# First sublayer of a long kernel: the inverse levels and u and w as 128-row products on a block diagonal

## The chip, the cores and the metric

The kernel runs on one core of one Trainium2 chip. The metric is the device time of one execution in microseconds, the median of several runs; less is better. Within the core, TensorE (PE; its weight loads are listed as PEld), VectorE (DVE), ScalarE (ACT), GpSimd (POOL) and SyncE (SP) each work through a queue of their own and meet at semaphores.

## The reference, cut to what matters

The reference is a chain of twelve sublayers, each followed by a layer norm. The change lies in the first, a gated delta rule over 4 batches, 256 times and 4 heads of 32 channels, in chunks of 32 times:

```python
A = jnp.where(tri_strict, -(kbc @ jnp.swapaxes(kc, -1, -2)), 0.0)
M = eye - A
T = solve_triangular(M, jnp.broadcast_to(eye, M.shape), lower=True)
u = T @ vc
w = T @ kbc
...
def step(S, inp):                      # over the 8 chunks
    attn = jnp.where(causal, q_i @ jnp.swapaxes(k_i, -1, -2), 0.0)
    u_adj = u_i - w_i @ S
    o_i = q_i @ S + attn @ u_adj
    return (S + jnp.swapaxes(k_i, -1, -2) @ u_adj, o_i)
```

So for each of 8 chunks, 4 batches and 4 heads, 128 small problems in all, a 32x32 unit lower triangular matrix is inverted, and the inverse is applied to v and k.

## The kernel before, in words

The program goes through the sublayers one after another. The first, `gated_delta`, has three parts, each closed by a barrier of all engines (`Place.close`, L66): `delta_project` (projections, convolutions and filters), `delta_inverse` (the part that changes) and `delta_scan` (the loop over the chunks).

In `delta_inverse` the 8 chunks are two groups g of four chunks; each group has four PSUM banks, `ps[g]`. Rows of a tile are (batch b, time i), its columns (head h, time j) or (h, channel), each 4 times 32. The order on every engine is the order of the code. The steps:

- Three sets of 8 transposes (L690) and their evictions on ScalarE (L747) give k, kb and vb with times in the rows.
- The Gram products (L698, L700): for every chunk, head and batch two 32x32 TensorE products, 128 per group. ScalarE copies `raw` (L750), GpSimd multiplies it by a mask for each of four levels into `A_s` (L767), VectorE makes the first `invT` (L775 to L778).
- Four levels. In each, for g = 0 and 1: four transposes of `invT` (L707), 64 products `A_s` by `invT` of 32x32 (L713); ScalarE evicts the turned `inv` (L754) and the product `M1` (L755); then for g = 0 and 1 64 products `inv` by `M1` (L722), and VectorE adds them to `invT` (L783), which the next level waits for.
- u: 64 products of 32x32 for each group (L731). w: 64 more (L739). ScalarE (L757, L758) and VectorE (L785, L786) evict one group each.

Every fp32 product of the code shows as two MATMUL and two LDWEIGHTS records in the trace, every transpose as one of each. In the trace the tiles are called `tiles_...` (this part), `delta_...` (shared by the three) and `scan_...`; `tiles_M` is `M1`.

`delta_scan` follows with 16 products of 32x32 each for the state (L856), the output (L862), w (L844) and q (L849) of every chunk; VectorE updates u (L902) and the state (L906, at first L908).

Of the kernel before, what the change touches and what calls it, by code (L numbers as in the profile page):

```python
# [633 lines left out]
def delta_inverse(m, kT, kqT, vbT, u, k, wT, attnT):  # L634
# [5 lines left out]
    LEVELS = 5  # L640
    with ExitStack() as ctx:
# [7 lines left out]
        M1 = place.sbuf("M1", [P, CH, P])  # L649
# [8 lines left out]
        A_ready = place.counter("A_ready")  # L658
        invT_ready = place.counter("invT_ready")
        M_made = place.counter("M_made")  # L660
        M_ready = place.counter("M_ready")
        U_made = place.counter("U_made")
        u_made = place.counter("u_made")
# [10 lines left out]
        def out_of(g, lo, hi):  # L674

            return ps[g][:, :, lo:hi].rearrange("p h (c j) -> p c h j", j=32)

# [9 lines left out]
        def _(pe):  # L687
# [4 lines left out]
            for g in range(2):  # L692
# [9 lines left out]
                mm.then_inc(grams_made.sem, 1)  # L702
            for s in range(1, LEVELS):
                for g in range(2):
                    pe.wait_ge(invT_ready.sem, invT_ready.nth(2 * (s - 1) + g + 1))
                    for n, c in enumerate(of(g)):
                        pe.transpose(ps[g][:, n, 2 * P:3 * P], invT[:, c, :], m.ident[:, :])  # L707
                    pe.wait_ge(A_ready.sem, A_ready.nth(2 * (s - 1) + g + 1))
                    for n, c in enumerate(of(g)):
                        for b in range(B):  # L710
                            for h in range(H):
                                on, to = slice(32 * b, 32 * b + 32), slice(32 * h, 32 * h + 32)
                                mm = pe.matmul(ps[g][to, b, 32 * n:32 * n + 32], A_s[on, s, c, to], invT[on, c, to], start=True, stop=True,  # L713
                                               skip_group_check=True)
                    mm.then_inc(M_made.sem, 1)
                for g in range(2):
                    pe.wait_ge(M_ready.sem, M_ready.nth(2 * (s - 1) + g + 1))
                    for n, c in enumerate(of(g)):
                        for h in range(H):
                            for b in range(B):  # L720
                                on, to = slice(32 * h, 32 * h + 32), slice(32 * b, 32 * b + 32)
                                mm = pe.matmul(ps[g][to, h, P + 32 * n:P + 32 * n + 32], inv[on, c, to], M1[on, c, to], start=True, stop=True,  # L722
                                               skip_group_check=True)
                    mm.then_inc(U_made.sem, 1)
            for g in range(2):
                pe.wait_ge(invT_ready.sem, invT_ready.nth(2 * (LEVELS - 1) + g + 1))
                for n, c in enumerate(of(g)):
                    for h in range(H):
                        for b in range(B):
                            on, ch = slice(32 * b, 32 * b + 32), slice(32 * h, 32 * h + 32)  # L730
                            mm = pe.matmul(ps[g][on, n, ch], invT[on, c, ch], vb[on, c, ch], start=True, stop=True, skip_group_check=True)  # L731
                mm.then_inc(u_made.sem, 1)
            for g in range(2):
                pe.wait_ge(u_made.sem, u_made.nth(g + 1))
                for n, c in enumerate(of(g)):
                    for b in range(B):
                        for h in range(H):
                            on, ch = slice(32 * b, 32 * b + 32), slice(32 * h, 32 * h + 32)
                            mm = pe.matmul(ps[g][ch, b, P + 32 * n:P + 32 * n + 32], kb[on, c, ch], invT[on, c, ch], start=True, stop=True,  # L739
                                           skip_group_check=True)  # L740
                mm.then_inc(w_made.sem, 1)

        @block.scalar
        def _(act):
# [3 lines left out]
            for g in range(2):  # L748
                act.wait_ge(grams_made.sem, grams_made.nth(g + 1))
                act.activation(by32(raw, g), out_of(g, 0, P), ACT.Copy).then_inc(raw_ready.sem, 1)  # L750
            for s in range(1, LEVELS):
                for g in range(2):
                    act.wait_ge(M_made.sem, M_made.nth(2 * (s - 1) + g + 1))
                    act.activation(inv[:, 4 * g:4 * g + 4, :], ps[g][:, :, 2 * P:3 * P], ACT.Copy)  # L754
                    act.activation(by32(M1, g), out_of(g, 0, P), ACT.Copy).then_inc(M_ready.sem, 1)  # L755
            act.wait_ge(w_made.sem, w_made.nth(1))
            act.activation(u[:, 0:4, :], ps[0][:, :, 0:P], ACT.Copy)  # L757
            act.activation(by32(wT, 0), out_of(0, P, 2 * P), ACT.Copy)  # L758

        @block.gpsimd  # L760
        def _(pool):
            pool.wait_ge(const_in.sem, const_in.nth(32))
# [7 lines left out]
        def _(dve):  # L770
            dve.wait_ge(const_in.sem, const_in.nth(32))
            for g in range(2):
# [6 lines left out]
                                  ALU.add).then_inc(invT_ready.sem, 1)  # L779
            for s in range(1, LEVELS):  # L780
                for g in range(2):
                    dve.wait_ge(U_made.sem, U_made.nth(2 * (s - 1) + g + 1))
# [3782 lines left out]
```

## Time and profile before

| | us |
|---|---|
| median of three runs | 3913.87 |
| lowest, highest | 3901.09, 3919.18 |
| the profiled execution, its own time | 3946.06 |
| its span in the trace | 3944.3 |
| mean granted TensorE clock in it | 0.892 of full |
| `delta_inverse`, first transpose to last copy | 99.1 to 195.1 |

All starts are microseconds from the start of the span. A row in order of time gives start, length, engine, line, tiles, the count of instructions merged in it, and in brackets how long the engine had been idle before and what ended that. "issue" there means that the engine waited for nothing that the profile shows. In tables of stretches PEclk is the granted clock as a share of full: 1.00 is 2.4 GHz, 0.50 is 1.2 GHz. The lengths of MATMUL records are modelled and overlap, so that the starts tell more than the ends.

### The profile page before, as it was taken

What the parts mean: (1) busy time and instruction counts of PE and PEld (TensorE: products, weight loads), DVE (VectorE), ACT (ScalarE), POOL (GpSimd) and SP (SyncE); (2) the same over time, 40 slices, a digit from 0 to 9 for tenths busy, and PEclk for the clock granted to TensorE, in tenths of its full rate; (3) what the DMA queues carried; (4) which work ended last, traced back from release to release, by engine and by line L of the source; (5) the groups of instructions that cost most, each with busy time, mean ns of one, the idle gap of its engine ahead of it and who ended that gap; (6) DMA issues with size and microseconds to landing.
All of it is one profiled execution on the core that took longest, in us unless ns stands there. A gap on an engine that the chain in (4) does not pass through costs nothing. (4 is left out here: it accounts for less than half of the span.)

```text
span 3944.3 us, 96221 instructions
## 1 busy us (share of the span) xinstructions
PE 3325.7 (84%) x40498; PEld 2328.4 (59%) x40498; DVE 2616.4 (66%) x4510; ACT 1952.2 (49%) x3525; POOL 1267.1 (32%) x842
## 2 busy tenths in 40 slices
PE   7566697999999998766649668999999988999996
PEld 4445665777777776731123345666666665667774
DVE  5124385666666666379977777888888864567773
ACT  1122344655555554359961234566665652345553
POOL 1101303555555553410021236655666631000000
PEclk9577888999999999788868889999999996789997
DMA  1021501000000000810000211111111101000000
GB/s 40 6 63 50 166 1 39 1 10 1 10 1 1 1 1 8 257 58 1 1 5 1 60 58 44 48 54 42 51 52 42 26 21 40 9 19 20 11 2 11
DMA packets 88726, 131.40 MB, mean 33 GB/s; under 512 B 18450, under 2 KB 60106, under 8 KB 87532
## 3 DMA queue, kind: packets, MB, share of 16 engines
q1 hardware_dynamic: 85292, 119.03, 10.6%
q8 instruction: 324, 5.31, 0.6%
q0 software_dynamic: 3008, 6.23, 0.4%
q14 instruction: 102, 0.84, 0.1%
HBM read 86.63 MB, written 10.94 MB: 25 GB/s over the span
## 5 line engine op out<-in xcount | busy, mean ns | idle before, releaser
L2786 POOL TENSOR_TENSOR wide_probs<-wide_probs,wide_factor 128x1024 f32<-128x1024 f32 x128 | 239.6, 1893 | 311.1 <-ACT wide_factor L2747 311.1
L2743 ACT ACTIVATE wide_probs<-wide_ps_s,wide_nm 128x1024 f32<-128x1024 f32 (+1 forms) x256 | 237.2, 927 | 172.6 <-DVE wide_nm L2828 152.8
L175 POOL TENSOR_TENSOR model_Y<-model_Y,model_X 128x512 f32<-128x512 f32 x12 | 15.2, 1268 | 942.4 <-POOLq L66 942.4
L2294 ACT ACTIVATE narrow_probsT<-narrow_ps 128x512 f32<-128x512 f32 (+1 forms) x448 | 220.1, 582 | 136.0 <-PE narrow_ps L2198 133.6
L2823 DVE TENSOR_REDUCE wide_nm<-wide_ps_s 128x1 f32<-128x1024 f32 x128 | 156.0, 1219 | 193.6 <-PE wide_ps_s L2629 193.6
L2348 DVE TENSOR_REDUCE narrow_part<-narrow_ps 128x1 f32<-128x512 f32 x384 | 242.4, 685 | 52.6 <-PE narrow_ps L2181 50.2
L3933 POOL TENSOR_TENSOR local_turn<-local_turn 128x1024 f32<-128x1024 f32 x96 | 226.7, 2369 | 157.0 <-DVE local_turn L3991 156.8
L3147 DVE TENSOR_TENSOR bonds_strain<-peri_in_moved 128x1664 f32<-128x1664 f32 (+3 forms) x128 | 257.0, 2085 | 1.0 <-PEq L66 1.0
L3198 PE MATMUL bonds_ps<-bonds_act_of,bonds_out 128*32 128x448 f32 (+3 forms) x1024 | 153.5, 697 | 117.9 <-ACT bonds_act_of L3171 83.9
L2181 PE MATMUL narrow_ps<-second_KQ 32*128 32x512 f32 x768 | 247.2, 668 | 1.1 <-ACT second_KQ L2265 1.0
L2641 PE MATMUL wide_ps<-model_ident,wide_probs 128*128 128x128 f32 (+1 forms) x1664 | 238.9, 274 | 10.8 <-DVE wide_probsT L2833 9.1
L2833 DVE COPY wide_probsT<-wide_ps 128x512 f32<-128x512 f32 x256 | 173.7, 686 | 84.8 <-PE wide_ps L2641 84.0
L2198 PE MATMUL narrow_ps<-narrow_Q,second_KQ 32*128 32x256 f32 (+1 forms) x1664 | 227.8, 396 | 0.0
L2629 PE MATMUL wide_ps_s<-wide_KQ 64*128 64x512 f32 (+1 forms) x1024 | 212.3, 531 | 9.9 <-ACT wide_probs L2743 9.0
L2641 PEld LDWEIGHTS wide_ps<-model_ident,wide_probs 128*128 128x128 f32 (+1 forms) x1664 | 193.3, 139 | 42.7 <-DVE wide_probsT L2833 13.6
L3942 POOL TENSOR_TENSOR local_turn<-local_turn,local_ss 128x1024 f32<-128x1024 f32 x96 | 184.1, 1918 | 82.5 <-ACT local_ss L3877 82.5
L3814 PE MATMUL local_ps<-e_wqkv,local_xs 128*128 128x512 f32 x384 | 193.0, 627 | 4.9 <-DVE local_xs L3965 4.3
L2653 PE MATMUL wide_ps<-wide_probsT,wide_V 128*64 128x128 f32 (+1 forms) x3328 | 195.9, 275 | 0.9 <-DVE wide_probsT L2833 0.9
L2198 PEld LDWEIGHTS narrow_ps<-narrow_Q,second_KQ 32*128 32x128 f32 (+1 forms) x1664 | 175.2, 182 | 25.6 <-DVE narrow_part L2348 7.7
L2653 PEld LDWEIGHTS wide_ps<-wide_probsT,wide_V 128*64 128x64 f32 (+1 forms) x3328 | 180.5, 137 | 5.4 <-DVE wide_probsT L2833 1.1
L3198 PEld LDWEIGHTS bonds_ps<-bonds_act_of,bonds_out 128*32 128x32 f32 x1024 | 25.4, 123 | 240.5 <-ACT bonds_act_of L3171 179.2
L2629 PEld LDWEIGHTS wide_ps_s<-wide_KQ 64*128 64x128 f32 x1024 | 93.4, 187 | 95.1 <-issue 93.3
(643 smaller groups left out, 8452.0 us busy)
## 6 DMA issues: line engine op xcount, KB each, us to landing
moe_w<-in_L_ffn_w SPq DMA_DIRECT2D x62, 512.0 KB
local_V<-local_V SPq DMA_DIRECT2D x96, 128.0 KB
e_wqkv<-in_L_ffn_qkv SPq DMA_DIRECT2D x6, 1536.0 KB, 7.2
local_V<-local_V SPq DMA_DIRECT2D x144, 64.0 KB
context_rows<-in_ctx SPq DMA_DIRECT2D x8, 768.0 KB
e_keys<-in_ctx_T SPq DMA_DIRECT2D x6, 800.5 KB, 4.9
e_source<-in_ctx_T SPq DMA_DIRECT2D x4, 800.5 KB, 4.4
second_source<-in_ctx_T SPq DMA_DIRECT2D x4, 800.5 KB, 5.7
```

What stands on the lines that cost most here:

```text
L2181: mm = pe.matmul(bank[:, 0:hi - lo], Qh[:, t * P:(t + 1) * P], Kh[:, lo:hi], start=True, stop=True)
L2198: mm = pe.matmul(bank[0:hi - lo, at:at + q1 - q0], KQ_of(s)[part_of(h), lo:hi], Q2[part_of(h), s % RING, q0:q1], start=True, stop=True, sk ...
L2294: act.activation(probsT[0:high, c % PROBS, h, 0:wide], bank[0:high, 0:wide], ACT.Exp).then_inc(t_taken_act.sem, 1)
L2348: dve.tensor_reduce(part[:, s % 2, t, h, piece:piece + 1], bank[:, :], AX.X, ALU.min).then_inc(s_taken.sem, 1)
L2629: mm = pe.matmul(ps_s[h][:, j * BANK:j * BANK + c1 - c0], KQ[rows, s % 2, pair, K + tile * P:K + (tile + 1) * P], KQ[rows, s % 2, pair, c0 ...
L2641: mm = pe.transpose(bank[0:high(c), j * P:(j + 1) * P], probs[:, n % 2, h, c * P:c * P + high(c)], m.ident[:, :])
L2653: mm = pe.matmul(bank[64 * h:64 * h + 64, 0:P], V[0:high(c), s % 2, c, 128 * pair + 64 * h:128 * pair + 64 * h + 64], probsT[0:high(c), n ...
L2743: act.activation(probs[:, n % 2, h, lo:hi], ps_s[h][:, 0:hi - lo], ACT.Exp, bias=nm[:, n % 2, h, 2 * half:2 * half + 1], scale=1.0, accum_ ...
L2786: pool.tensor_tensor(v, v, factor[:, n // 4 % 2, j:j + 1].broadcast_to([P, CUT]), ALU.mult).then_inc(lowered[i].sem, 1)
L3147: dve.tensor_tensor(out, window, here, ALU.subtract).then_inc(strain_dve.sem, 1)
L3814: mm = pe.matmul(slot[:, j, :], xs[:, b, WIN + u * P:WIN + (u + 1) * P], wqkv[:, i, at + j * BANK:at + (j + 1) * BANK], start=True, stop=True)
L3933: pool.tensor_tensor(turn1[:, n % 2, j, :, :], turn1[:, n % 2, j, :, :], turn2[:, j, :, :], ALU.add)
```

## The change

The two products of each level, and u and w, are formed by contracting over all 128 rows. For that, one operand is held four times as wide, with its 32-row pieces set apart on a block diagonal and zeros elsewhere. `invT4[:, c, h, :]` is 128x128 and holds head h's four batch pieces of `invT`; `M4[:, c, b, :]` likewise holds the product. GpSimd clears both tiles once (two memsets of 128x4096 fp32).

- Each level's first product is 16 products per group instead of 64, of `A_s[:, s, c, ch]` (128 rows, 32 columns, stationary) with `invT4[:, c, h, :]` (128 columns, moving), all to bank MID of the group. The second is 16 of `inv[:, c, on]` with `M4[:, c, b, :]`, all to bank OUT. The transposes of `invT` stay and go to bank TURN.
- Filling the tiles that are set apart is new work: after every update of `invT`, VectorE copies the pieces b = 0, 1 and ScalarE the pieces b = 2, 3, for each group; after every first product, VectorE copies h = 0, 1 out of PSUM into `M4` and ScalarE h = 2, 3. Each copy has 32 partitions of 512 elements. They take the place of the eviction of `M1`, one instruction of 128 partitions.
- u is formed turned (`uT`), 16 products per group, evicted by VectorE, turned back with four transposes per group, and evicted again. w is 16 products per group, and its eviction is a plain copy.
- The Gram products and the scan are as they were.

The core of the diff:

```diff
+        invT4 = place.sbuf("invT4", [P, CH, H, P])
+        M4 = place.sbuf("M4", [P, CH, B, P])
+        uT = place.sbuf("uT", [P, CH, P])
+        def bank(g, k):
+            return ps[g][:, k, :].rearrange("p (c x) -> p c x", x=P)
+        def apart(v, g, i):
+            own = slice(32 * i, 32 * i + 32)
+            return v[own, 4 * g:4 * g + 4, :, own]
+        def parts(v, i):
+            return v[32 * i:32 * i + 32].rearrange("p c (x j) -> p c x j", j=32)
...
         def _(pe):
+            def against_invT4(g, k, left):
+                for n, c in enumerate(of(g)):
+                    for h in range(H):
+                        ch = slice(32 * h, 32 * h + 32)
+                        mm = pe.matmul(bank(g, k)[ch, n, :], left[:, c, ch], invT4[:, c, h, :], start=True, stop=True, skip_group_check=True)
+                return mm
             for s in range(1, LEVELS):
                 for g in range(2):
                     pe.wait_ge(invT_ready.sem, invT_ready.nth(2 * (s - 1) + g + 1))
                     for n, c in enumerate(of(g)):
-                        pe.transpose(ps[g][:, n, 2 * P:3 * P], invT[:, c, :], m.ident[:, :])
+                        mm = pe.transpose(bank(g, TURN)[:, n, :], invT[:, c, :], m.ident[:, :])
+                    mm.then_inc(inv_made.sem, 1)
                     pe.wait_ge(A_ready.sem, A_ready.nth(2 * (s - 1) + g + 1))
-                        for b in range(B):
-                            for h in range(H):
-                                on, to = slice(32 * b, 32 * b + 32), slice(32 * h, 32 * h + 32)
-                                mm = pe.matmul(ps[g][to, b, 32 * n:32 * n + 32], A_s[on, s, c, to], invT[on, c, to], start=True, stop=True,
+                    pe.wait_ge(invT4_dve.sem, invT4_dve.nth(2 * (s - 1) + g + 1))
+                    pe.wait_ge(invT4_act.sem, invT4_act.nth(2 * (s - 1) + g + 1))
+                    against_invT4(g, MID, A_s[:, s]).then_inc(M_made.sem, 1)
+                for g in range(2):
+                    pe.wait_ge(inv_ready.sem, inv_ready.nth(2 * (s - 1) + g + 1))
+                    pe.wait_ge(M4_dve.sem, M4_dve.nth(2 * (s - 1) + g + 1))
+                    pe.wait_ge(M4_act.sem, M4_act.nth(2 * (s - 1) + g + 1))
                     for n, c in enumerate(of(g)):
                         for b in range(B):
+                            on = slice(32 * b, 32 * b + 32)
+                            mm = pe.matmul(bank(g, OUT)[on, n, :], inv[:, c, on], M4[:, c, b, :], start=True, stop=True, skip_group_check=True)
                     mm.then_inc(U_made.sem, 1)
...
+                against_invT4(g, OUT, vb).then_inc(uT_made.sem, 1)
+                against_invT4(g, MID, kb).then_inc(w_made.sem, 1)
+            for g in range(2):
+                pe.wait_ge(uT_ready.sem, uT_ready.nth(g + 1))
                 for n, c in enumerate(of(g)):
+                    mm = pe.transpose(bank(g, TURN)[:, n, :], uT[:, c, :], m.ident[:, :])
...
         def _(act):
+            act.wait_ge(cleared.sem, cleared.nth(2))
+            def spread_invT(s, g):
+                act.wait_ge(invT_ready.sem, invT_ready.nth(2 * s + g + 1))
+                for b in range(2, B):
+                    ins = act.activation(apart(invT4, g, b), parts(group(invT, g), b), ACT.Copy)
...
         def _(pool):
+            pool.memset(invT4[:, :, :, :], 0.0).then_inc(cleared.sem, 1)
+            pool.memset(M4[:, :, :, :], 0.0).then_inc(cleared.sem, 1)
...
         def _(dve):
+            for g in range(2):
+                spread_invT(g)
             for s in range(1, LEVELS):
                 for g in range(2):
+                    dve.wait_ge(M_made.sem, M_made.nth(2 * (s - 1) + g + 1))
+                    for h in range(2):
+                        ins = dve.tensor_copy(apart(M4, g, h), parts(bank(g, MID), h))
+                    ins.then_inc(M4_dve.sem, 1)
+                for g in range(2):
                     dve.wait_ge(U_made.sem, U_made.nth(2 * (s - 1) + g + 1))
-                    dve.tensor_tensor(by32(invT, g), by32(invT, g), out_of(g, P, 2 * P), ALU.add).then_inc(invT_ready.sem, 1)
+                    dve.tensor_tensor(group(invT, g), group(invT, g), bank(g, OUT), ALU.add).then_inc(invT_ready.sem, 1)
+                    spread_invT(g)
```

On TensorE, the last level and u and w of the kernel before (`ps0` and `ps1` are the banks of the two groups, a count is of products of the code, and the shape is that of the result, partitions by columns):

```order
L707 MATMUL tiles5_ps0<-model1_ident,tiles5_invT 128x128 x4
L713 MATMUL tiles5_ps0<-tiles5_invT,tiles5_A_s 32x32 x64
L707 MATMUL tiles5_ps1<-model1_ident,tiles5_invT 128x128 x4
L713 MATMUL tiles5_ps1<-tiles5_invT,tiles5_A_s 32x32 x64
L722 MATMUL tiles5_ps0<-tiles5_M1,tiles5_inv 32x32 x64
L722 MATMUL tiles5_ps1<-tiles5_M1,tiles5_inv 32x32 x64
L731 MATMUL tiles5_ps0<-tiles5_vb,tiles5_invT 32x32 x64
L731 MATMUL tiles5_ps1<-tiles5_vb,tiles5_invT 32x32 x64
L739 MATMUL tiles5_ps0<-tiles5_invT,tiles5_kb 32x32 x64
L739 MATMUL tiles5_ps1<-tiles5_invT,tiles5_kb 32x32 x64
```

The same place in the changed kernel:

```order
L741 MATMUL tiles5_ps0<-model1_ident,tiles5_invT 128x128 x4
L734 MATMUL tiles5_ps0<-tiles5_invT4,tiles5_A_s 32x128 x16
L741 MATMUL tiles5_ps1<-model1_ident,tiles5_invT 128x128 x4
L734 MATMUL tiles5_ps1<-tiles5_invT4,tiles5_A_s 32x128 x16
L754 MATMUL tiles5_ps0<-tiles5_M4,tiles5_inv 32x128 x16
L754 MATMUL tiles5_ps1<-tiles5_M4,tiles5_inv 32x128 x16
L734 MATMUL tiles5_ps0<-tiles5_invT4,tiles5_vb 32x128 x16
L734 MATMUL tiles5_ps0<-tiles5_invT4,tiles5_kb 32x128 x16
L734 MATMUL tiles5_ps1<-tiles5_invT4,tiles5_vb 32x128 x16
L734 MATMUL tiles5_ps1<-tiles5_invT4,tiles5_kb 32x128 x16
L764 MATMUL tiles5_ps0<-model1_ident,tiles5_uT 128x128 x4
L764 MATMUL tiles5_ps1<-model1_ident,tiles5_uT 128x128 x4
```

The order of the steps within a level is the same, every 64 have become 16, and the two sets of transposes of `uT` stand behind the last products.

On ScalarE, one level and the start of the next in the changed kernel (`32x16x32` is a copy of 32 partitions by 512 elements into a tile that is set apart); before, the four rows of a level were L754, L755, L754, L755:

```order
L780 ACTIVATE tiles5_invT4<-tiles5_invT 32x16x32 x4
L788 ACTIVATE tiles5_inv<-tiles5_ps0 128x512
L791 ACTIVATE tiles5_M4<-tiles5_ps0 32x16x32 x2
L788 ACTIVATE tiles5_inv<-tiles5_ps1 128x512
L791 ACTIVATE tiles5_M4<-tiles5_ps1 32x16x32 x2
```

A level has 10 ScalarE instructions where it had 4, and on VectorE 10 (two adds L841, four copies of `invT` L828, four of the product L837) where it had 2.

## Rows read from the trace of the kernel before

**Rows 1.** The profile's page: the span and the instructions.

```profile
span 3944.3 us, 96221 instructions
```

**Rows 2.** Table of stretches: us, busy time by engine with counts, PEclk, DMA.

```profile
core 0: us, PE busy (x) PEld busy (x) DVE busy (x) ACT busy (x) POOL busy (x), PEclk, DMA share, GB/s
...
99.00:196.00 97.00, 53.89 (x3153) 47.03 (x3161) 11.83 (x17) 14.03 (x23) 10.32 (x8) 0.54 0.02 5
```

**Rows 3.** The same table, in finer stretches of the changed stage.

```profile
103.70:108.70 5.00, 3.34 (x280) 3.12 (x280) 0.00 (x0) 1.13 (x2) 0.00 (x0) 1.00 0.03 7
...
196.00:222.00 26.00, 15.27 (x928) 12.52 (x925) 4.04 (x14) 0.09 (x1) 0.62 (x1) 0.50 0.03 7
```

**Rows 4.** Order of time, TensorE: start, length, line, tiles, count, idle before it.

```profile
126.46 1.57 PE L722 MATMUL tiles_ps<-tiles_M,tiles_inv 32*32 32x32 f32 x128 [2.16 <-issue]
130.46 1.18 PE L722 MATMUL tiles_ps<-tiles_M,tiles_inv 32*32 32x32 f32 x92 [2.43 <-issue]
131.57 1.11 PE L707 MATMUL tiles_ps<-model_ident,tiles_invT 128*128 128x128 f32 x4
132.62 0.41 PE L713 MATMUL tiles_ps<-tiles_invT,tiles_A_s 32*32 32x32 f32 x32
134.19 1.22 PE L713 MATMUL tiles_ps<-tiles_invT,tiles_A_s 32*32 32x32 f32 x96 [1.16 <-issue]
```

**Rows 5.** DMA queues, stretch 99 to 196 us: packets, MB, share of 16 engines.

```profile
q8 instruction: 24, 0.39, 1.7%
```

**Rows 6.** Order of time, VectorE.

```profile
118.47 1.71 DVE L778 TENSOR_TENSOR tiles_invT<-tiles_invT,tiles_ident 128x512 f32<-128x512 f32 x1
...
142.94 0.69 DVE L783 TENSOR_TENSOR tiles_invT<-tiles_invT,tiles_ps 128x512 f32<-128x512 f32 x1 [10.56 <-PE tiles_ps L722]
...
158.80 0.69 DVE L783 TENSOR_TENSOR tiles_invT<-tiles_invT,tiles_ps 128x512 f32<-128x512 f32 x1 [11.17 <-PE tiles_ps L722]
...
194.40 0.68 DVE L786 COPY delta_wT<-tiles_ps 128x512 f32<-128x512 f32 x1
...
197.60 0.29 DVE L902 TENSOR_TENSOR delta_u<-delta_u,scan_ps_w 128x128 f32<-128x128 f32 x1 [0.86 <-PE scan_ps_w L844]
```

**Rows 7.** Order of time, ScalarE and then GpSimd.

```profile
135.44 0.60 ACT L754 ACTIVATE tiles_inv<-tiles_ps 128x512 f32<-128x512 f32 x1 [10.41 <-PE tiles_ps L713]
135.94 0.59 ACT L755 ACTIVATE tiles_M<-tiles_ps 128x512 f32<-128x512 f32 x1
...
109.53 1.26 POOL L767 TENSOR_TENSOR tiles_A_s<-tiles_raw,tiles_levels 128x512 f32<-128x512 f32 x1 [62.83 <-ACT tiles_raw L750]
117.15 9.05 POOL L767 TENSOR_TENSOR tiles_A_s<-tiles_raw,tiles_levels 128x512 f32<-128x512 f32 x7 [6.35 <-ACT tiles_raw L750]
```

**Rows 8.** Order of time, TensorE: products of 128 rows by 32 columns elsewhere.

```profile
591.35 1.93 PE L2220 MATMUL narrow_ps_o<-narrow_probsT,narrow_V 128*32 128x256 f32 x16
...
601.62 1.07 PE L2220 MATMUL narrow_ps_o<-narrow_probsT,narrow_V 128*32 128x256 f32 x16
```

**Rows 9.** Stretches around each of these, and of the bond products (last row).

```profile
591.00:593.40 2.40, 2.40 (x19) 0.78 (x18) 1.53 (x3) 1.86 (x4) 0.00 (x0) 0.53 0.00 0
601.60:602.60 1.00, 1.00 (x17) 0.42 (x16) 1.00 (x3) 0.96 (x2) 0.00 (x0) 1.00 0.00 0
1742.00:1765.00 23.00, 11.17 (x100) 1.89 (x96) 23.00 (x14) 22.93 (x27) 0.00 (x0) 1.00 0.00 1
```

**Rows 10.** Groups by shape: busy us, mean ns; of VectorE, ScalarE and GpSimd.

```profile
L1652 DVE COPY moe_gT<-moe_ps_x 8x512 f32<-8x512 f32 x2 | 1.3, 674 | 1.5 <-PE moe_ps_x L1731 1.5
...
L3966 DVE COPY layers_Z<-model_XT 128x1024 f32<-128x1024 f32 x1 | 0.7, 695 | 0.0
...
L2290 ACT ACTIVATE narrow_probsT<-narrow_maskedT 128x512 f32<-128x512 f32 x64 | 40.3, 630 | 60.2 <-DVE narrow_maskedT L2364 59.9
...
L2106 POOL MEMSET narrow_V<- 128x4992 f32 x1 | 4.3, 4257 | 0.2 <-issue 0.2
```

**Rows 11.** Order of time, TensorE, in the scan: idle before the state products.

```profile
206.62 0.34 PE L856 MATMUL scan_ps_s<-delta_u,delta_k 32*32 32x32 f32 x15 [1.15 <-issue]
```

More of the change, by code:

```diff
@@ L640, in delta_inverse @@
     LEVELS = 5
+    MID, OUT, TURN = 0, 1, 2
     with ExitStack() as ctx:
@@ L658, in delta_inverse @@
         A_ready = place.counter("A_ready")
+        cleared = place.counter("cleared")
         invT_ready = place.counter("invT_ready")
+        invT4_dve = place.counter("invT4_dve")
+        invT4_act = place.counter("invT4_act")
+        inv_made = place.counter("inv_made")
+        inv_ready = place.counter("inv_ready")
         M_made = place.counter("M_made")
-        M_ready = place.counter("M_ready")
+        M4_dve = place.counter("M4_dve")
+        M4_act = place.counter("M4_act")
         U_made = place.counter("U_made")
+        uT_made = place.counter("uT_made")
+        uT_ready = place.counter("uT_ready")
         u_made = place.counter("u_made")
@@ L676, in out_of, with group @@
             return ps[g][:, :, lo:hi].rearrange("p h (c j) -> p c h j", j=32)
+        def group(v, g):
+            return v[:, 4 * g:4 * g + 4, :]
+        def bank(g, k):
[5 more added lines that the diff above has]
+            return v[32 * i:32 * i + 32].rearrange("p c (x j) -> p c x j", j=32)
         def mask(s):
@@ L732, in _ @@
                 mm.then_inc(u_made.sem, 1)
[L733 to L741, printed above, removed]
@@ L779, in _, with spread_invT @@
                                   ALU.add).then_inc(invT_ready.sem, 1)
+            dve.wait_ge(cleared.sem, cleared.nth(2))
+            def spread_invT(g):
+                dve.drain()
+                for b in range(2):
+                    ins = dve.tensor_copy(apart(invT4, g, b), parts(group(invT, g), b))
+                ins.then_inc(invT4_dve.sem, 1)
+            for g in range(2):
+                spread_invT(g)
             for s in range(1, LEVELS):
                 for g in range(2):
-                    dve.wait_ge(U_made.sem, U_made.nth(2 * (s - 1) + g + 1))
-                    dve.tensor_tensor(by32(invT, g), by32(invT, g), out_of(g, P, 2 * P), ALU.add).then_inc(invT_ready.sem, 1)
-            dve.wait_ge(w_made.sem, w_made.nth(2))
-            dve.tensor_copy(u[:, 4:8, :], ps[1][:, :, 0:P])
-            dve.tensor_copy(by32(wT, 1), out_of(1, P, 2 * P))
+                    dve.wait_ge(M_made.sem, M_made.nth(2 * (s - 1) + g + 1))
+                    for h in range(2):
+                        ins = dve.tensor_copy(apart(M4, g, h), parts(bank(g, MID), h))
+                    ins.then_inc(M4_dve.sem, 1)
+                for g in range(2):
+                    dve.wait_ge(U_made.sem, U_made.nth(2 * (s - 1) + g + 1))
+                    dve.tensor_tensor(group(invT, g), group(invT, g), bank(g, OUT), ALU.add).then_inc(invT_ready.sem, 1)
+                    spread_invT(g)
+            for g in range(2):
+                dve.wait_ge(uT_made.sem, uT_made.nth(g + 1))
+                dve.tensor_copy(group(uT, g), bank(g, OUT)).then_inc(uT_ready.sem, 1)
+            dve.wait_ge(u_made.sem, u_made.nth(2))
+            dve.tensor_copy(group(u, 1), bank(1, TURN))
 def delta_scan(m, kqT, k, u, wT, attnT, gates, total):
```

35 lines of the change are left out of this document (15 added, 20 removed).

## The prediction

> **What bounds the kernel now.** I read the table of stretches first [rows 1, 2]: the part that changes lies between 99 and 196 us, 97 of 3944 us, in which VectorE, ScalarE and GpSimd are busy for 12, 14 and 10 us. The gain can only come from TensorE there, and TensorE is busy for 54 of the 97. So the question is what it does in the other 43.
>
> The rows in order of time tell it [rows 4]. A full run of 128 MATMUL records of L722 starts at 126.46 and the next one at 130.46, 4.00 us apart, but the records of one take 1.57 us; then the engine is idle for 2.43 us and waits for nothing. The stop does not stand between groups of work: L713 issues 32 records from 132.62, stops for 1.16 us and issues 96 more. It comes after every 128 MATMUL records, which with their 128 weight loads are 256 instructions. The queue that brings instructions moved 24 packets and 0.39 MB in these 97 us [rows 5], so 16 KB each, one packet in 4.0 us. I read this as: TensorE's instructions arrive in blocks of 256, a block takes 3.5 to 4.0 us to come, and a stretch of tiny products uses one up in 1.6 us. The stage goes at the speed of its instruction count. From one add of group 0 to the next is 158.80 - 142.94 = 15.86 us [rows 6], for 256 products and 8 transposes, 1040 instructions or 4.06 blocks: 3.9 us each.
>
> (The Trainium skill, "Runtime: NRT & Kernel Launch", section "Instruction fetch mechanics", also has blocks of 256 instructions, but says that crossing one is mostly hidden because the sequencer dispatches more slowly than blocks arrive. The first half agrees with the 128 records between two stops, the second does not with 2.43 us idle of 4.00. If the rule held, the idle time would be something else; that is the third rival.)
>
> **What the change removes.** On TensorE, 4 levels of 256 products become 4 of 64, and the 256 of u and w become 64 plus 8 transposes. In instructions, four for each product and two for each transpose: 4 x 1040 + 1024 = 5184 before, 4 x 272 + 272 = 1360 after. That is 15 blocks fewer. 1.06 blocks in a level want 4.2 us, and by the sum below a level lasts over 6 us, so that the next block comes while TensorE waits for others. I cost the fetch at nothing there; its cover is the copying of ScalarE and VectorE.
>
> **What a product costs now.** The trace of before has such products elsewhere, 128 rows by 32 columns, four in a row to the four column strips: 16 records of 256 moving columns take 1.93 us at the half clock and 1.07 us at the full one [rows 8, 9]. In columns this is just one new burst (16 products, 32 records of 128). The last record's latency is in it, so a next burst can start some 0.3 us earlier: 1.7 and 0.85 us. The four transposes of a group hold the next product off for 132.62 - 131.57 = 1.05 us at the half clock [rows 4]; I take half at the full one.
>
> **What the copies cost.** A copy of few partitions is as long as a wide one: 674 ns for 8x512 out of PSUM on VectorE [rows 10]. So a piece of 32x512 costs what 128x512 costs: VectorE out of PSUM 0.69, ScalarE 0.60 with the next start 0.49 behind [rows 7], ScalarE out of SBUF 0.63 [rows 10]. VectorE out of SBUF: 128x1024 in 695 ns [rows 10], half of that is 0.35; the upper bound is 0.69 if the pieces spoil that speed. I take 0.35; the upper end adds 0.7 to a pair, and is still covered, since ScalarE's pair takes 1.1.
>
> **One level, worked out as a chain.** Time 0 is the end of the add for group 0. VectorE spreads it (two copies into `invT4`) until 0.8 and adds group 1 until 1.6; ScalarE spreads group 0 until 1.2 and group 1 until 2.8.
> At the half clock TensorE is the longest: first burst of group 0 from 1.35 (the transposes lie under the spreading), transposes of group 1 and its burst 3.05 to 5.8, second burst of group 0 until 7.5, its latency and the hop 0.5, the add 0.69: 8.7 us. Under it ScalarE evicts `inv` and writes `M4` of group 0 until 4.4, VectorE until 4.6, and group 1's until 7.5, just in time for the last burst.
> At the full clock ScalarE's queue is the longest: spreads until 2.8, `inv` and `M4` of group 0 until 4.4, burst 0.85, hop 0.3, add 0.69 and hops: 6.4 us.
> The new waits stand at the head of TensorE's queue: the first burst of a group waits for both engines' spreading, and behind it stand the other group's transposes and everything else. For such waits that stack up I add 0.4 and 0.5 us: 9.1 and 6.9 us in place of 15.86.
>
> **The ends.** Before, from the end of the first `invT` of group 1 (118.47 + 1.71 = 120.18) to the end of the last copy (194.40 + 0.68 = 195.08) are 74.9 us [rows 6].
> - Start: VectorE can spread group 0 only after that `invT`, and L778 took 1.71 instead of 0.69 us while GpSimd was at the masks, which run until 126.2 [rows 6, 7]. Four spreading copies meet the same: 1.5 us, from 0 to 4. TensorE's first burst waits for them where L713 did not.
> - Four levels: 36.4 us all at the half clock, 27.6 all at the full one.
> - u and w: 4 bursts, a copy of `uT`, 8 transposes, last eviction: 11 or 7 us. The last level's spreading is in it.
> - The two memsets on GpSimd: 4096/4992 of 4.26 us [rows 10] is 3.5 each, so some 99 to 106; the first mask starts at 109.53 [rows 7]. Free.
>
> **Which clock.** TensorE has the half clock in the whole second half of the stage and in the scan [rows 2, 3], with 15.3 of 26 us busy in tiny products. With bursts over all four strips, busy 11.2 of 23 us, it stayed at the full clock elsewhere [rows 9]. The new level is of this second kind, at least 50% busy. It begins at the half clock. I take the first level at 9.1, three at 7.4 (mostly full), u and w at 8.5: 1.5 + 9.1 + 22.2 + 8.5 = 41.3 us. Gain 74.9 - 41.3 = 33.6 us.
>
> **Behind it.** The scan too stops once a chunk for 1.15 us with nothing to wait for [rows 11], one block for every chunk. It stays as it is; but TensorE arrives with its blocks fetched instead of in the middle of a shortage: a gain of 0 to 3.5 us, I take 1.5. In all -35 us. The profiled execution took 3946.1 us and the median is 3913.9; the 32 us between them lie elsewhere, and I subtract the same 35 from the median: 3879. With everything at the half clock, 1.5 + 36.4 + 11 = 48.9, the gain is 26; all at the full one it is 39 and with the scan 42.
>
> **Rivals.**
> 1. *The chain of copies becomes the bound and is longer than summed.* A level has six hand-overs between engines, and 20 instructions on ScalarE and VectorE instead of 6. If each hand-over costs 0.6 us more than I took, a level is 12 us and the gain 75 - (4 + 48 + 12) = 11, within 0.5%: 3903. For it: 0.86 us go by in the scan between two VectorE instructions around one small burst [rows 6]. Against it: that is a hop both ways with 16 products in it, about 0.2 us per hop. (The Trainium skill, "TensorEngine Tiling (Array Packing)", section "PSUM Bottleneck", says that after such a speed-up the eviction may become the bottleneck and that both engines should share it, as they do here; no row shows it for these tiles.)
> 2. *Slower: the 32-column products don't overlap.* At the half clock four records together take 1.7 / 8 = 0.213 us; one by one, a burst is 32 of these, 6.8 us; a level is 4 x 6.8 + 2.1 = 29.3 us against 15.9, u and w 29 against 15: 3914 + 54 + 14 = 3982. It decides as soon as less than 2 of 4 overlap at that clock (a burst over 3.5 us). Against it: [rows 8], where four do, in one bank as here.
> 3. *No change: the idle time belongs to each burst, not to each 256 instructions.* If each of the 20 bursts kept 2.2 us, 44 us come on top of 41 and the stage is as long as now, or 10 us longer: 3914 to 3924. Against it: the stop in the middle of L713 [rows 4].
>
> **How the numbers follow.** About 0.5% (20 us) is what a measurement of this kernel can tell from no change. Forecast (gain 20 to 45): 0.81. Rival 1, 0.11, of which a third is still above 20 us. Rival 2, 0.03. Rival 3, 0.03. The remaining 0.02 are that the clock moves elsewhere and hides or doubles the result. Faster 0.85, same 0.11, slower 0.04. Range: the ends 42 and 20, with 6 us for the scatter of medians of three (the three runs lie 18 us apart): 3866 to 3900. It leaves out rivals 2, 3 and most of 1.
>
> **What would show it.** In the trace of after: the part from 99 us ends at about 161 instead of 195 us; the adds L841 of group 0 lie 6.5 to 9.5 us apart; the instruction queue moves about 0.15 MB for it, not 0.39; a burst of 32 records of L734 starts within 1.7 us (half clock) or 0.85 (full); "issue" in front of it is gone, and the names in front of it are ScalarE's and VectorE's. PEclk between 125 and 160 tells which of the two level times holds. I am wrong if a level stays over 11 us, if a burst takes over 3 us, or if the gain shows in this stage and is lost in the scan or later.

## The result, and the profile after

| | before | after |
|---|---|---|
| median | 3912.3 us (4 runs, 3901.1 to 3919.2) | 3868.5 us (4 runs, 3866.5 to 3885.8) |
| ratio | | 0.9896, interval 0.9866 to 0.9926 |
| the profiled execution's own time | 3946.1 | 3868.7 |
| `delta_inverse`, first transpose to last copy | 96.0 (99.1 to 195.1) | 58.9 (98.3 to 157.2) |
| the scan behind it, first product to the first VectorE instruction behind its chunks (L911, L972) | 27.1 | 27.9 |

The changed kernel is faster by 43.8 us, where 35 were forecast. The page of after begins:

```profile
span 3866.8 us, 92494 instructions
```

Against [rows 1], 3727 instructions are gone. In order of time, TensorE at the end of the stage (start, length, engine, line, tiles, count of records, idle before it):

```profile
150.21 1.08 PE L754 MATMUL tiles_ps<-tiles_M,tiles_inv 128*32 128x128 f32 x32 [0.75 <-ACT tiles_M L791]
151.65 1.08 PE L734 MATMUL tiles_ps<-tiles_invT,tiles_vb 128*32 128x128 f32 x32 [0.35 <-ACT tiles_invT L780]
152.52 1.08 PE L734 MATMUL tiles_ps<-tiles_invT,tiles_kb 128*32 128x128 f32 x32
...
161.63 0.27 PE L910 MATMUL scan_ps_s<-scan_state,delta_kqT 32*32 32x32 f32 x5 [2.01 <-issue]
...
165.13 0.28 PE L910 MATMUL scan_ps_s<-scan_state,delta_kqT 32*32 32x32 f32 x4 [1.44 <-issue]
```

Where [rows 4] had "issue" in front of the products, now ScalarE's copies stand there; the names `tiles_M` and `tiles_invT` are also those of `M4` and `invT4`. Two bursts in a row, for u and for w, start 152.52 - 151.65 = 0.87 us apart. "issue" comes back in the scan, with its own 32x32 products, 161.63 - 158.02 = 3.6 us after its start. The instruction queue for 97 to 160 us, against 24 packets and 0.39 MB [rows 5]:

```profile
q8 instruction: 10, 0.16, 1.1%
```

VectorE in order of time, from the first `invT` of group 1 on; L828 spreads `invT` into `invT4`, L837 writes `M4`, L841 is the add:

```profile
117.89 1.72 DVE L821 TENSOR_TENSOR tiles_invT<-tiles_invT,tiles_ident 128x512 f32<-128x512 f32 x1
119.69 5.54 DVE L828 COPY tiles_invT<-tiles_invT 32x512 f32<-32x512 f32 x4
125.27 1.38 DVE L837 COPY tiles_M<-tiles_ps 32x512 f32<-32x512 f32 x2
127.48 1.38 DVE L837 COPY tiles_M<-tiles_ps 32x512 f32<-32x512 f32 x2 [0.84 <-PE tiles_ps L734]
128.89 0.69 DVE L841 TENSOR_TENSOR tiles_invT<-tiles_invT,tiles_ps 128x512 f32<-128x512 f32 x1
129.67 0.84 DVE L828 COPY tiles_invT<-tiles_invT 32x512 f32<-32x512 f32 x2
...
135.65 0.69 DVE L841 TENSOR_TENSOR tiles_invT<-tiles_invT,tiles_ps 128x512 f32<-128x512 f32 x1 [0.46 <-PE tiles_ps L754]
...
142.58 0.69 DVE L841 TENSOR_TENSOR tiles_invT<-tiles_invT,tiles_ps 128x512 f32<-128x512 f32 x1 [0.46 <-PE tiles_ps L754]
```

From one add of group 0 to the next are 6.76 and 6.93 us where [rows 6] had 15.86. But the first add of group 0 comes 128.89 - 119.61 = 9.28 us after the end of group 1's first `invT`: the first four spreading copies took 5.54 us, a pair later 0.84. TensorE's first burst waits for them:

```profile
122.52 1.94 PE L734 MATMUL tiles_ps<-tiles_invT,tiles_A_s 128*32 128x128 f32 x32 [5.62 <-DVE tiles_invT L828]
```

GpSimd's rows say what ran beside them:

```profile
98.28 3.51 POOL L803 MEMSET tiles_invT<- 128x4096 f32 x1 [52.98 <-POOLq L66]
...
116.57 9.80 POOL L810 TENSOR_TENSOR tiles_A_s<-tiles_raw,tiles_levels 128x512 f32<-128x512 f32 x7 [5.57 <-ACT tiles_raw L774]
```

One steady level of ScalarE (L780 spreads, L788 is `inv`, L791 writes `M4`):

```profile
136.37 1.26 ACT L780 ACTIVATE tiles_invT<-tiles_invT 32x512 f32<-32x512 f32 x2 [0.17 <-DVE tiles_invT L841]
138.20 1.26 ACT L780 ACTIVATE tiles_invT<-tiles_invT 32x512 f32<-32x512 f32 x2 [0.57 <-DVE tiles_invT L841]
139.49 0.60 ACT L788 ACTIVATE tiles_inv<-tiles_ps 128x512 f32<-128x512 f32 x1
140.11 1.19 ACT L791 ACTIVATE tiles_M<-tiles_ps 32x512 f32<-32x512 f32 x2
141.32 0.60 ACT L788 ACTIVATE tiles_inv<-tiles_ps 128x512 f32<-128x512 f32 x1
141.94 1.19 ACT L791 ACTIVATE tiles_M<-tiles_ps 32x512 f32<-32x512 f32 x2
143.30 1.26 ACT L780 ACTIVATE tiles_invT<-tiles_invT 32x512 f32<-32x512 f32 x2 [0.17 <-DVE tiles_invT L841]
```

It works for 2 x (1.26 + 0.60 + 1.19) = 6.1 of the 6.93 us, without a gap from 138.20 to 143.13. Last, the table of stretches (busy time with counts of PE, PEld, DVE, ACT and POOL, then the granted clock):

```profile
120.00:127.00 7.00, 4.48 (x66) 3.80 (x70) 6.49 (x6) 3.26 (x6) 6.37 (x5) 0.50 0.00 0
127.00:157.40 30.40, 23.61 (x618) 18.80 (x608) 23.77 (x41) 23.60 (x39) 0.00 (x0) 0.99 0.01 3
158.00:186.00 28.00, 13.67 (x928) 11.95 (x928) 4.16 (x16) 1.02 (x1) 0.62 (x1) 0.56 0.03 7
```

The clock came back to full at about 127 us, at the end of the first level.

**How much of the result is the change.** In the two profiled executions the same instructions can be set beside each other. GpSimd's last instruction of this sublayer (L175, `model_Y`) starts at 239.26 us before and 202.20 after. So the two traces are 37.1 us apart there, then 31 at 600 us of after, 28 at 2000, 23 at 3290. Behind that, in a part that the change does not touch, 55 us more appear, 45 of them before 3443 us. The first 26 arise in one stretch, which is this in the kernel before:

```profile
3309.10:3370.60 61.50, 61.20 (x292) 40.01 (x285) 28.10 (x124) 18.30 (x39) 0.00 (x0) 0.50 0.01 2
```

and the same work in the changed kernel:

```profile
3286.30:3321.40 35.10, 34.25 (x285) 23.65 (x284) 27.39 (x124) 17.74 (x40) 0.00 (x0) 1.00 0.02 4
```

The granted clock differs there, 0.50 and 1.00. It is the chip's scatter from one execution to the next, as the first experiment shows, and not a part of the gain. What belongs to the change is 36 to 37 us at the end of the sublayer.

### The profile page after: what moved, and what is told of

It reads as the page before. It is cut to its first block and busy times, and to the rows that moved or that the text cites. A ratio compares the mean times of both kernels' runs of the same rounds, so it can differ in the third digit from the quotient of the medians.

```text
span 3866.8 us, 92494 instructions
## 1 busy us (share of the span) xinstructions
PE 3266.6 (84%) x38586; PEld 2285.0 (59%) x38586; DVE 2639.8 (68%) x4547; ACT 1970.1 (51%) x3554; POOL 1275.3 (33%) x844
## 5 line engine op out<-in xcount | busy, mean ns | idle before, releaser
L175 POOL TENSOR_TENSOR model_Y<-model_Y,model_X 128x512 f32<-128x512 f32 x12 | 15.2, 1269 | 930.9 <-POOLq L66 930.9
```

## The experiments

Every kernel is the changed one with the edit shown. Times of the parts are from each run's trace; the kernel before ran beside each set, with medians of 3906.5 us (experiments 1 to 4) and 3904.8 us (5 to 8). Experiments 2, 3, 6 and 8 are one run each.

**1. The changed kernel again**, no edit.

> The changed kernel once more, in five rounds beside the kernel before. If the gain is only what the stage gives in the trace (96.0 us from the first transpose to the last copy before, 58.9 after: 37.1, less 0.9 lost in the scan), the medians lie 36 us apart, ratio 0.991. The theory that something later in the program gains too (the median of the first four runs moved by 44) expects 44 or more, ratio 0.989 or less. The level period in its trace is 6.9 us again if the full clock in the levels is caused by the bursts, and up to 9.1 in some level if it is luck.

Measured: 3873.7 us (7 runs, 3860.2 to 3902.9), ratio 0.9889 (0.9852 to 0.9927), a gain of 32.7 us by the medians. Stage 59.7 us, periods of a level 6.75, 6.94, 6.93, scan 27.1. At the end of the sublayer it stands 37.1 us ahead of the profiled execution of before. Yet its own time is 3902.9 us, 34 us above that of the first profiled execution of the same kernel. At 3276 us of the first one it is 3.7 us ahead of it, at 3856 us 34.2 behind. Its row for the stretch of 35.10 us above, with the half clock that the kernel before had there:

```profile
3282.30:3343.90 61.60, 61.30 (x293) 40.17 (x287) 27.99 (x124) 18.30 (x39) 0.00 (x0) 0.50 0.01 2
```

So the stage repeats to 0.8 us and the scatter of the total is that of the clock late in the program. That is why the experiments below are read by the length of the stage and of its parts, not by their totals.

**2. As many instructions as before, in the new structure.**

```diff
+            def pad(g):
+                for n, c in enumerate(of(g)):
+                    for b in range(3):
+                        for h in range(H):
+                            on, to = slice(0, 32), slice(32 * h, 32 * h + 32)
+                            pe.matmul(ps[g][to, 3, 96 * n + 32 * b:96 * n + 32 * b + 32], kb[on, c, to], vb[on, c, to], start=True, stop=True, skip_group_check=True)
...
                     against_invT4(g, MID, A_s[:, s]).then_inc(M_made.sem, 1)
+                    pad(g)
...
                     mm.then_inc(U_made.sem, 1)
+                    pad(g)
```

> The changed kernel with 48 more tiny products (32x32, from kb and vb, into a bank that nothing reads) behind each of the 16 bursts of the levels, so that a level has the instruction count of the kernel before, 1040 instead of 272. Nothing that other engines wait for is changed. Theory (instructions arrive in blocks of 256, 3.5 to 4.0 us each): a level takes 4.06 blocks, 15 to 16 us instead of 6.93, with stops of TensorE after every 128 MATMUL records. Rival (the time before was that of the products themselves or of the hand-overs): 48 tiny products add at most 0.7 us at the full clock and 1.3 at the half one, a level is 9 to 11 us.

Measured: 3899.6 us, stage 93.5 us, periods 14.2, 15.3, 15.7: two of the three are back at the 15.3 to 15.9 of the kernel before. TensorE in order of time, with the stop inside a burst of the new products (L762 is the second product, L742 the padding):

```profile
146.27 1.02 PE L742 MATMUL tiles_ps<-tiles_vb,tiles_kb 32*32 32x32 f32 x96
147.22 0.86 PE L762 MATMUL tiles_ps<-tiles_M,tiles_inv 128*32 128x128 f32 x24
149.34 0.43 PE L762 MATMUL tiles_ps<-tiles_M,tiles_inv 128*32 128x128 f32 x8 [1.26 <-issue]
```

The stop divides a burst into 24 and 8 records, where nothing is waited for. At 0.95 us for a padding of 96 records (147.22 - 146.27), 0.87 for a burst and 0.6 for four transposes, a level has 8.5 us of work at the full clock. At the half clock, by the starts from 139.77 to 144.12 us (1.44 for a padding, 1.87 for a burst, 1.04 for the transposes), it has 15.3 us. The padding costs more than the 0.7 and 1.3 us of the expectation. Three rows of stretches, one for each period,

```profile
131.80:146.00 14.20, 14.20 (x524) 11.54 (x520) 5.76 (x10) 6.05 (x10) 0.00 (x0) 0.55 0.02 5
146.00:161.30 15.30, 12.54 (x533) 9.63 (x523) 5.76 (x10) 6.05 (x10) 0.00 (x0) 0.78 0.02 4
161.30:177.00 15.70, 14.00 (x527) 11.04 (x520) 5.76 (x10) 6.05 (x10) 0.00 (x0) 0.67 0.02 4
```

show the first, 14.2, at nearly the half clock and busy throughout, so that one was bound by the products. The other two had the higher clock, were idle for 2.8 and 1.7 us, and took longer still, as long as the work at the half clock alone or longer: there the products are not the bound, their number of instructions is. Their stops, where one shows, start 3.8 us or a multiple of it apart (149.34, 153.17, 160.88, 164.72, 176.36). This experiment confirms the count for these two, and shows that at the half clock the padded products come close to the same time by themselves.

**3. The strips one after another.** The loops over chunks and strips changed places, so that eight records in a row go to one column strip.

```diff
-                for n, c in enumerate(of(g)):
-                    for h in range(H):
+                for h in range(H):
+                    for n, c in enumerate(of(g)):
                         ch = slice(32 * h, 32 * h + 32)
...
-                    for n, c in enumerate(of(g)):
-                        for b in range(B):
+                    for b in range(B):
+                        for n, c in enumerate(of(g)):
```

> The changed kernel with the loops of each burst turned round, so that four products in a row go to the same 32 columns of the array and not to four different ones. Same products, same counts. Theory (four products run side by side only if they stand next to each other in the queue): a burst of 32 records goes from 0.87 us to about 3.4 at the full clock, a level from 6.93 to 15 or more, the stage is about 40 us longer. Rival (the queue reaches far enough to run them side by side all the same): the burst stays under 1.5 us and the level under 9.

Measured: 3884.9 us, stage 75.2 us, 16.3 more than after; level 9.90 us. Both expectations missed. In order of time:

```profile
134.13 2.46 PE L734 MATMUL tiles_ps<-tiles_invT,tiles_A_s 128*32 128x128 f32 x32
136.52 0.66 PE L741 MATMUL tiles_ps<-model_ident,tiles_invT 128*128 128x128 f32 x4
```

and the stretch of this kernel:

```profile
128.00:170.00 42.00, 41.92 (x608) 39.47 (x605) 22.87 (x41) 22.95 (x38) 0.00 (x0) 1.00 0.01 2
```

A burst takes 136.52 - 134.13 = 2.39 us instead of 0.87, and TensorE is busy 41.9 of 42 us at the full clock: it has become the bound. So the order of the products is worth a factor of 2.7 here, where full overlap against none would be 4; whether the eight in a row overlap in part was not measured by itself. The mechanism of the second rival is real, but it takes another loop order to bring it about, and at the full clock even that costs 16 us and leaves the stage shorter than the 96.0 us of before.

**4. Spreading early.** GpSimd makes the masks of group 0 first and waits before the later masks of group 1; VectorE and ScalarE spread group 0 as soon as its `invT` is there, not after group 1's.

```diff
-            for s in range(1, LEVELS):
-                for g in range(2):
+            for g in range(2):
+                for s in range(1, LEVELS):
...
+                    if s == 2 and g == 1:
+                        pool.wait_ge(invT4_dve.sem, invT4_dve.nth(2))
...
                                   ALU.add).then_inc(invT_ready.sem, 1)
+                spread_invT(g)
```

> The changed kernel, but the first spreading of group 0 stands right behind its invT on VectorE and ScalarE, GpSimd makes all masks of group 0 first, and waits for the first spreading of group 1 before it makes the last three masks of group 1. Theory: in the changed kernel TensorE waits 5.6 us for four VectorE copies that take 5.54 us beside GpSimd instead of 1.7, so the first burst moves from 122.5 to about 117 us and the stage is 5 us shorter (54 instead of 58.9), the total about 5 us below the changed kernel. Rival: the start is hidden behind something else (the half clock lasts longer, a block of instructions is not there yet): under 2 us.

Measured: 3870.7 us (6 runs, 3863.1 to 3880.4), ratio 0.9889 (0.9852 to 0.9925). Stage 52.2 us, 6.7 less than after, where 5 were expected; the first add comes 4.4 us after the first `invT` of group 1, not 9.3. VectorE in order of time, group 0 beside the masks and group 1 without them:

```profile
111.91 2.71 DVE L817 COPY tiles_invT<-tiles_invT 32x512 f32<-32x512 f32 x2
...
118.16 0.85 DVE L817 COPY tiles_invT<-tiles_invT 32x512 f32<-32x512 f32 x2
```

The stage gave 6.7 us; the scan took 29.0 instead of 27.9 and gave 1.1 back. The medians differ by 3 us from the changed kernel's in the same set, less than their scatter.

**5. GpSimd takes a piece**, on top of 4: GpSimd copies b = 3 of every spreading of `invT`, ScalarE only b = 2.

```diff
-                for b in range(2, B):
+                for b in range(2, 3):
...
+                pool.tensor_copy(apart(invT4, g, 3), parts(group(invT, g), 3)).then_inc(invT4_pool.sem, 1)
```

> The early variant (masks in the order of groups, spreading right after each first invT), and GpSimd copies the piece b = 3 of every spreading of invT, so that ScalarE has four copies out of PSUM, two inv evictions and two spreading copies in a level instead of ten instructions. If ScalarE's queue (6.1 of 6.93 us busy) sets the period, a level goes down by 0.6 to 1.2 us, to 5.7 to 6.3 us, and the stage by 2.5 to 5 us against early (52.2). If the rival holds (GpSimd's copy is slower than the two that it stands in for and takes VectorE's port), the period is 7 us or more, and VectorE's copies out of SBUF last longer than 0.42 us.

Measured: 3860.4 us (6 runs, 3851.7 to 3866.3), ratio 0.9875 (0.9847 to 0.9903), stage 51.8 us, period 6.79 us instead of 6.94, scan 26.9. Neither range of the expectation was met, a part of each reading holds: ScalarE is relieved, but VectorE then has this level (the first row is of the first level, beside the masks):

```profile
119.42 2.89 DVE L852 COPY tiles_M<-tiles_ps 32x512 f32<-32x512 f32 x4
...
129.14 0.69 DVE L856 TENSOR_TENSOR tiles_invT<-tiles_invT,tiles_ps 128x512 f32<-128x512 f32 x1
129.92 1.18 DVE L834 COPY tiles_invT<-tiles_invT 32x512 f32<-32x512 f32 x2
131.13 0.69 DVE L856 TENSOR_TENSOR tiles_invT<-tiles_invT,tiles_ps 128x512 f32<-128x512 f32 x1
131.91 1.18 DVE L834 COPY tiles_invT<-tiles_invT 32x512 f32<-32x512 f32 x2
133.12 2.78 DVE L852 COPY tiles_M<-tiles_ps 32x512 f32<-32x512 f32 x4
```

It is busy 6.5 of 6.79 us and waits for nobody. Its pair out of SBUF takes 1.18 us, with GpSimd's copy of 0.86 us beside it, instead of 0.84. This fits ScalarE's queue as the bound, but the copy that relieves it lengthens VectorE's queue from 5.8 to 6.5 us a level, and 0.15 us is left of the 0.6 to 1.2 expected.

**6. The later masks after the first spreading.** Only GpSimd waits; everything else as in the changed kernel.

```diff
                     if s == 1:
                         pool.wait_ge(raw_ready.sem, raw_ready.nth(g + 1))
+                    if s == 2 and g == 0:
+                        pool.wait_ge(invT4_dve.sem, invT4_dve.nth(2))
```

> The changed kernel, but GpSimd multiplies the masks of levels 2 to 4 only after VectorE's four first spreading copies (they wait for invT4_dve), so that only the two masks of level 1 can meet them. It isolates the 5.54 us that the four copies took beside GpSimd. If GpSimd's work is the cause, the four take 1.7 to 2.5 us, the first add comes 3 to 4 us earlier after the first invT of group 1 (9.3 before), and the stage is about 55.5 us. If the copies are slow for their form (32 partitions, the first ones after the memsets), they stay at 5 us or more.

Measured: 3874.2 us, stage 57.6 us. In order of time, VectorE:

```profile
118.81 1.78 DVE L830 COPY tiles_invT<-tiles_invT 32x512 f32<-32x512 f32 x4
...
126.01 2.55 DVE L830 COPY tiles_invT<-tiles_invT 32x512 f32<-32x512 f32 x2
```

and GpSimd:

```profile
120.67 7.61 POOL L812 TENSOR_TENSOR tiles_A_s<-tiles_raw,tiles_levels 128x512 f32<-128x512 f32 x6 [2.69 <-DVE tiles_invT L830]
```

The four copies take 1.78 us when GpSimd is idle, so 3.8 of the 5.54 us came from GpSimd's work. The first add comes 6.5 us after the first `invT`, 2.8 earlier. But now the masks lie beside the next spreading, whose pair takes 2.55 us, and the first period is 8.46 instead of 6.76. Of 2.8 us won, 1.7 are lost again; the stage is only 1.3 us shorter, where 3.4 were expected.

**7. The levels alone**: u and w as before the change (the two loops of 128 products of 32x32 and their evictions put back).

> The changed kernel, but u and w are formed as before the change (256 small products of 32x32 and plain evictions; the last spreading of invT is left out, since nothing reads it). It splits the gain between levels and u and w. By the theory (TensorE's instructions come in blocks of 256, one per 3.5 to 4.0 us) the levels keep their periods of 6.75 to 6.95 us, and u and w, 1024 instructions, take four blocks again: from the last add of group 0 to the end of the stage 15 to 20 us (20.5 before, 7.7 in the changed kernel). Stage 67 to 71 us, of the 37 us gained 25 to 29 stay. By the rival (small products are slow only at the half clock, and the clock is full here) u and w take about 9 us and the stage 61.

Measured: 3873.2 us (8 runs, 3851.4 to 3902.5), ratio 0.9922 (0.9883 to 0.9961). Stage 64.6 us, the same periods 6.76, 6.94, 6.95, and 14.2 us from the last add of group 0 to the end (7.7 after, 20.5 before). That is just under the 15 to 20 of the theory and far over the 9 of the rival; the stage is shorter than the 67 to 71 expected. TensorE in order of time:

```profile
153.69 1.22 PE L762 MATMUL tiles_ps<-tiles_vb,tiles_invT 32*32 32x32 f32 x122 [1.13 <-issue]
...
157.15 1.47 PE L770 MATMUL tiles_ps<-tiles_invT,tiles_kb 32*32 32x32 f32 x128 [2.17 <-issue]
...
160.88 1.51 PE L770 MATMUL tiles_ps<-tiles_invT,tiles_kb 32*32 32x32 f32 x124 [2.26 <-issue]
```

The stops are back, 3.46 us apart at the full clock (until 157.5 us) and 3.73 at the half clock behind it. But there are three, not four; I read this as one block that had come during the levels, which no row shows by itself. Of the 37 us of the stage, the levels bring 31.3 and u and w 5.8.

**8. Half a block more ahead of the scan.**

```diff
+            for i in range(32):
+                on, to = slice(0, 32), slice(32 * (i % 4), 32 * (i % 4) + 32)
+                pe.matmul(ps[0][to, 3, 32 * (i // 16):32 * (i // 16) + 32], kb[on, 0, to], vb[on, 0, to], start=True, stop=True, skip_group_check=True)
```

> The changed kernel and 32 additional 32x32 products (128 instructions, half a block) at the end of TensorE's part of the stage, into an unused bank; nobody waits for them. They take TensorE 0.5 to 1 us under the last evictions. If the length of the scan depends on where the block boundaries lie in it, the stops (one per chunk, 1.4 to 2.0 us, before the first products of the output L910 in the changed kernel) move by half a chunk, to the products of the state or w, and the scan (27.9) changes by 1 to 4 us in either direction. If it doesn't, the stops stay before the same products and the scan stays within 0.5 us.

Measured: the time of the one run is 3858.2 us, within the scatter. The stops are at other products, as expected: L926, those with `attnT`, instead of L910, those with `kqT`. Behind the second one they come 3.9 to 4.2 us apart instead of 3.5 to 4.1:

```profile
170.22 0.33 PE L926 MATMUL scan_ps_w<-delta_u,delta_attnT 32*32 32x32 f32 x8 [1.59 <-issue]
...
174.14 0.34 PE L926 MATMUL scan_ps_w<-delta_u,delta_attnT 32*32 32x32 f32 x9 [1.59 <-issue]
```

The scan takes 29.2 us, 1.3 more than after. That does not show that the place of the boundary sets its length. In experiments 1, 2, 3, 4 and 6 the boundaries lie at the same records of the scan as in after: TensorE has as many products ahead of it, or in experiment 2 such as make 3072 more instructions, 12 whole blocks. Still the scan takes 27.1, 24.9, 24.3, 29.0 and 28.2 us. In experiment 4, for instance, the stop stands where it stands in after, behind 24 records of the products with `kqT`:

```profile
153.00 0.56 PE L908 MATMUL scan_ps_s<-scan_state,delta_kqT 32*32 32x32 f32 x24
155.70 0.28 PE L908 MATMUL scan_ps_s<-scan_state,delta_kqT 32*32 32x32 f32 x5 [2.15 <-issue]
```

Two other things differ. Experiments 2 and 3 have six stops instead of seven, the first 4.7 and 4.8 us after the scan's start instead of 3.6 to 3.9. And the stops of the five lie between 3.2 and 4.1 us apart: from the first to the last are 22.43 us in after and 21.61 in experiment 1, the same program, and that is the whole difference between their scans. What sets this distance stays open.

## Why the prediction was right, step by step

- **The bound.** Blocks of 256 instructions set the pace of the stage before; experiment 2 brings the old level back by instructions of no use (in two of its three periods; the first was bound by its products at the half clock), and experiment 7 brings the old stops back for u and w. Rival 3, idle time for each burst, falls: the bursts of after follow each other in 0.87 us. So does rival 2 at the half clock, where the bursts at 122.52 and 125.43 us take 1.86 and 1.71 us against 1.7 forecast.
- **The instructions.** Forecast 0.15 MB, measured 0.16. That fetching hides under the copies holds: no "issue" stands in front of a product from 127 to 157 us.
- **A level.** 6.9 us forecast at the full clock, 6.93 measured, and ScalarE's queue as its bound. The sum was right by two errors that cancel: ScalarE's two copies start 0.59 to 0.63 us apart, not 0.49, and VectorE's spreading copy takes 0.42, not 0.35; in return less was lost between engines than the 0.5 us added for waits that stack up. Rival 1, a level of 12 us, falls.
- **The clock.** I put the first level at the half clock and the others at 7.4 us, mostly full. It was at the half clock until 127 us, then full, so three levels took 20.6 us instead of 22.2.
- **The start** is the term that was mis-sized: 1.5 us, 0 to 4, for VectorE beside GpSimd's masks. Experiment 6 prices the copies at 3.8 us more, near the upper end, and experiment 4 shows that with the waiting around it 4.9 us (9.28 - 4.41) hung on it. The factor stood in the rows, 1.71 instead of 0.69 for one add, or 2.5; for the copies it was 3.1, and all four lie beside the masks. The start and the first level together, 9.28 + 0.69 = 9.97 us from `invT` to the end of the add, still came out 0.6 us below my 1.5 + 9.1. So the level had been put too high, which hid it. In experiment 6, with four copies in 1.78 us, both together take 6.51 + 0.69 = 7.2 us, at a mean clock of 0.67 from 118 to 125.2 us.
- **u and w.** 8.5 forecast, 7.0 measured from the end of the last add of group 0. The whole is 9.97 + 20.63 + 6.98 = 37.6 us against a forecast of 41.3.
- **The scan.** A gain of 1.5 us forecast, a loss of 0.8 measured. The step that failed is "TensorE arrives with its blocks fetched": the scan has seven stops after as before, the first 3.6 us after its start (3.8 before), so no block more was in store. The loss is in the distance of the stops, 22.43 us from the first to the last against 21.60 before. Experiments 2 and 3, with one stop fewer, show that the gain exists (24.9 and 24.3 us); why it comes in these two and not in the changed kernel stays open.
- **Sum.** 37.1 in the stage less 0.8 in the scan are 36.3, against 35 forecast. That they lie so close is in part luck: by the measure of the forecast the stage gave 74.9 - 37.6 = 37.3 us, 3.7 more than the 33.6, and the scan 2.3 less than forecast. The difference to the 43.8 of the medians lies in the scatter elsewhere; the second set gave 32.7.

(The Trainium skill, "Runtime: NRT & Kernel Launch", section "Instruction fetch mechanics", says that crossing a block is mostly hidden. Experiment 7 speaks against it for products as small as these: at the full clock their stop is 2.17 of 3.46 us.)

## What to carry to other kernels

Count TensorE's instructions in a stretch and divide by 256: if the blocks times 3.5 to 4 us come to more than the engines' work, fewer instructions are worth more than better products, and padding them back tests it. Before copies on VectorE are added, look at what GpSimd does in the same microseconds, and when a contention is moved away, look for where it goes. A gain of 1% in a program whose late clock scatters by 30 us is read from the stage's own length.

Of the variants with more than one run, number 5 has the lowest median, 3860.4 us. Its interval (0.9847 to 0.9903) overlaps the changed kernel's, so only its stage, 51.8 us against 58.9, is known to be better.

## What the runs showed of the hardware

- VectorE's copies from SBUF to SBUF took 3 times as long beside GpSimd's masks: 5.54 us for four, 1.78 without; 2.55 and 0.85 for two. Beside one GpSimd copy of 32x512 two take 1.18. Its copies out of PSUM hardly suffer: in experiment 5 four took 2.89 us beside the masks and 2.78 without. (The Trainium skill, "GPSIMD Engine Reference", section "1. Specifications", names SBUF interfaces that GpSimd shares with VectorE, with contention for VectorE instructions in a two-port mode or with two SBUF inputs. The trace agrees for the add with two SBUF inputs, 1.72 instead of 0.69 us. For a copy, 1.27 to 1.39 instead of 0.42 us, it gives the size, but no row shows the mode.)
- Copies of 32 partitions by 512 elements cost 0.60 to 0.69 us out of PSUM on either engine, as much as those of 128 partitions.
- The 32 records of a burst of 128 rows by 32 columns start within 0.87 us at the full clock when successive products go to different column strips, and within 2.39 us when eight in a row go to the same one.
- Blocks came 3.2 to 4.2 us apart, once 4.5 (experiment 8), in the stretches that were bound by them. The clock alone does not set it: 3.46 us at the full clock and 3.73 at the half clock in experiment 7, 3.46 to 3.47 at the half clock in the scan of before (199.69 to 213.55 us).
